# An adaLN transformer layer on 8 cores: every third load of the weight conversion is issued by GpSimd's queue instead of SyncE's

## The reference

```
mod = silu(c) @ wmod                        # six vectors of 1024 per sequence: sa, ca, ga, sb, cb, gb
h = layernorm(x) * (1 + ca) + sa
x = x + ga * attention(h)                   # causal, 8 heads of 128, k and v through a latent of 32
h = layernorm(x) * (1 + cb) + sb
x = x + gb * (shared(h) + routed(h))        # MoE: 8 experts, weights of the top 2; all are computed
shared / expert: (silu(h @ Wgate) * (h @ Wup)) @ Wdown     # 1024 -> 512 -> 1024
```

## Time and profile before

| | us |
|---|---|
| median of 3 runs | 1985.06 |
| all runs | 1984.98, 1985.06, 1988.2 |
| the profiled execution | 1989.04 |
| its span on the slowest core (core 7) | 1987.4 |
| spans of the 8 cores | 1967.9 to 1987.4 |

### The profile page before, as it was taken

How to read it: one execution, slowest core, us unless ns; L and a number is a source line. 1 busy time by engine, 2 the same in 40 slices (tenths; PEclk the granted TensorE clock), 3 DMA queues, 4 the chain that set the end, 5 groups by cost and what they waited for, 6 DMA issues and landing times.

```text
span 1987.4 us, 20612 instructions; the slowest of 8 cores (1967.9 to 1987.4 us)
## 1 busy us (share of the span) xinstructions
PE 1295.3 (65%) x5238; PEld 483.6 (24%) x5238; DVE 687.8 (35%) x1269; ACT 495.5 (25%) x914; POOL 216.1 (11%) x226
## 2 busy tenths in 40 slices
PE   3613245125677622537997998898814499999998
PEld 0111122110021100212332333333302233333333
DVE  0333322343124613323334333234453333443433
ACT  0031312320056324234332432243132210000000
POOL 0002020022345773000000000000000000000000
PEclk8855557557875655656998999899956699999999
DMA  9506040059978775000111112111100012211114
GB/s 276 160 0 187 16 149 11 0 180 281 301 238 246 227 225 165 1 0 22 43 64 64 33 53 64 43 64 64 64 0 1 0 64 75 75 64 64 64 64 190
DMA packets 90437, 193.99 MB, mean 98 GB/s; under 512 B 14184, under 2 KB 14248, under 8 KB 90328
## 3 DMA queue, kind: packets, MB, share of 16 engines
q1 hardware_dynamic: 64848, 130.64, 21.7%
q10 hardware_dynamic: 16648, 33.60, 5.5%
q0 software_dynamic: 8832, 28.45, 3.6%
HBM read 155.92 MB, written 36.70 MB: 97 GB/s over the span
## 4 chain that ended last, share of the span: by engine, by line
PE 57%; DVE 13%; issue 10%; ACT 9%; DMA 8%; DVEq 1%; ACTq 1%; POOL 0%; SPq 0%; POOLq 0%
PE ps L947 14%; PE ps L914 13%; PE ps L929 12%; DMA stage<-wmod 5%; PE ps L1085 4%; PE ps L549 3%; PE ps L450 3%; PE ps L1028 3%; ACT h1b L535 3%; DVE h1b L542 2%; DVE h1b L539 2%; DVE st_sm L502 2%; DMA q_aug<-bbf 2%; PE ps L703 2%; PE ps L604 1%
## 5 line engine op out<-in xcount | busy, mean ns | idle before, releaser
L947 PE MATMUL ps<-down_bf,act_e 128*128 128x512 bf16 x1152 | 288.3, 384 | 34.6 <-DVE act_e L937 12.8
L914 PE MATMUL ps<-hT,gate_bf 128*128 128x512 bf16 x1152 | 285.0, 392 | 19.8 <-ACT r_t L883 13.8
L549 PE MATMUL ps<-ident,h1b 128*128 128x128 f32 x256 | 69.1, 425 | 322.6 <-DVE h1b L542 322.6
L929 PE MATMUL ps<-hT,up_bf 128*128 128x512 bf16 x1152 | 274.8, 382 | 1.4 <-PE ps L914 0.7
L937 DVE TENSOR_TENSOR act_e<-ps,silu_s 128x512 bf16<-128x512 f32 x144 | 99.6, 692 | 419.1 <-PE ps L929 377.5
L956 DVE SCALAR_TENSOR_TENSOR x_res<-ps,comb,x_res 128x512 f32<-128x512 f32 x256 | 192.2, 751 | 147.1 <-PE ps L947 143.5
L923 ACT ACTIVATE silu_s<-ps 128x512 bf16<-128x512 f32 x144 | 86.1, 598 | 516.9 <-PE ps L914 516.8
L1090 ACT ACTIVATE pT<-ps 128x512 bf16<-128x512 f32 (+3 forms) x320 | 159.3, 533 | 159.9 <-PE ps L1085 147.4
L914 PEld LDWEIGHTS ps<-hT,gate_bf 128*128 128x128 bf16 x1152 | 112.9, 100 | 168.4 <-issue 46.4
L947 PEld LDWEIGHTS ps<-down_bf,act_e 128*128 128x128 bf16 x1152 | 96.5, 97 | 221.3 <-issue 144.7
L929 PEld LDWEIGHTS ps<-hT,up_bf 128*128 128x128 bf16 x1152 | 113.0, 99 | 143.5 <-issue 12.0
(11 more groups left out here) (117 smaller groups left out, 833.1 us busy)
## 6 DMA issues: line engine op xcount, KB each, us to landing
stage<-wmod ACTq DMA_DIRECT2D x96, 256.0 KB, 10.8
gate_bf<-wc_g SPq DMA_DIRECT2D x72, 256.0 KB, 4.7
up_bf<-wc_u SPq DMA_DIRECT2D x72, 256.0 KB, 3.4
down_bf<-wc_d SPq DMA_DIRECT2D x72, 256.0 KB, 3.6
pc_in<-w_gate SPq DMA_DIRECT2D x64, 256.0 KB, 5.8
pc_in<-w_up SPq DMA_DIRECT2D x64, 256.0 KB, 4.5
pc_in<-w_down SPq DMA_DIRECT2D x32, 512.0 KB, 4.0
wc_g<-pc_o POOLq DMA_DIRECT2D x36, 256.0 KB, 5.0
```

Of the source, the lines that this page charges most:

```text
L549: tok = P.op("t", lambda e, dc=dc, u=u, pt=pt: e.transpose(pt[:, 128 * u:128 * (u + 1)], h1b[:, 128 * dc:128 * (dc + 1)], ident32[:]), rd= ...
L914: tok = P.op("t", lambda e, buf=buf, hc=hc, qc=qc, dc=dc, psg=psg: e.matmul(psg[:, :], gate_bf[:, buf, dc, 128 * hc:128 * (hc + 1)], hT[:, ...
L929: tok = P.op("t", lambda e, hc=hc, qc=qc, dc=dc, psu=psu: e.matmul(psu[:, :], up_bf[:, dc, 128 * hc:128 * (hc + 1)], hT[:, dc, 512 * qc:51 ...
L947: tok = P.op("t", lambda e, i=i, dch=dch, hc=hc, psd=psd: e.matmul(psd[:, :], act_e[:, hc, 128 * i:128 * (i + 1)], down_bf[:, hc, 512 * dc ...
```

## The change

Unit n takes its load's issuing engine from n mod 3: with n mod 3 = 2 it is POOL ("g"), otherwise SP ("q") as before. Nothing else differs: same transfers, same buffers, same semaphores, same waits.

```diff
--- before.py
+++ after.py
@@ -371,17 +371,18 @@
         def _pc_unit(kind, e_, u):
             islot = _pci[0] % 3
             oslot = _pci[0] % 2
+            qe = "g" if _pci[0] % 3 == 2 else "q"
             _pci[0] += 1
             bi, bo = b_pcin[islot], b_pcout[oslot]
             war = list(bi.r) + ([bi.w] if bi.w else [])
             if kind == "d":
                 if e_ < E:
-                    t_in = P.dma("q", lambda e, e_=e_, u=u, islot=islot: e.dma_start(
+                    t_in = P.dma(qe, lambda e, e_=e_, u=u, islot=islot: e.dma_start(
                         out=pc_in[:, islot, :],
                         in_=dwdown[e_, 128 * u:128 * (u + 1), :]),
                         extra=war, sem="P%d" % islot, serial=False)
                 else:
-                    t_in = P.dma("q", lambda e, u=u, islot=islot: e.dma_start(
+                    t_in = P.dma(qe, lambda e, u=u, islot=islot: e.dma_start(
                         out=pc_in[:, islot, :],
                         in_=dwsd[128 * u:128 * (u + 1), :]),
                         extra=war, sem="P%d" % islot, serial=False)
@@ -391,13 +392,13 @@
                 for h2 in range(2):
                     dc = 2 * u + h2
                     if e_ < E:
-                        t_in = P.dma("q", lambda e, e_=e_, dc=dc, h2=h2, islot=islot,
+                        t_in = P.dma(qe, lambda e, e_=e_, dc=dc, h2=h2, islot=islot,
                                      dsrc=dsrc: e.dma_start(
                             out=pc_in[:, islot, 512 * h2:512 * (h2 + 1)],
                             in_=dsrc[e_, 128 * dc:128 * (dc + 1), :]),
                             extra=war, sem="P%d" % islot, serial=False)
                     else:
-                        t_in = P.dma("q", lambda e, dc=dc, h2=h2, islot=islot,
+                        t_in = P.dma(qe, lambda e, dc=dc, h2=h2, islot=islot,
                                      dsrcs=dsrcs: e.dma_start(
                             out=pc_in[:, islot, 512 * h2:512 * (h2 + 1)],
                             in_=dsrcs[128 * dc:128 * (dc + 1), :]),
```

## The result

| | before | after |
|---|---|---|
| median of 10 runs, us | 1985.28 | 2051.8 |
| profiled execution, us | 1989.04 | 2051.83 |
| its spans on the 8 cores, us | 1967.9 to 1987.4 | 2025.7 to 2050.2 |

The change makes the kernel 3.2% slower: the ratio is 1.0319, 95% interval 1.0305 to 1.0333. The direction and the mechanism held. The size was put at 35 us; it is 67 by the medians and 63 by the ratio, near the upper end of the range.

The account below looks back on a forecast made before the run. The conversion was taken as off the path with 53 us to spare; lengthened rounds bring up_bf at 866 us, a 37.5 us stall less 2.65, net 35, so 1985.06 becomes 2020 us, range 1988 to 2056.

Parts of the forecast that it names:

- the slack: Before PE first uses up_bf at 828.5 us: converted weights are there at 775.5 us, 53 us to spare.
- The loads of wq and wo: On SP behind conversion loads: pushed by at most 16 us each, against slack of 51 and 17 us; costed at nothing.
- A late load is exposed: On POOL, every third load is issued right ahead of its cast and waited for: 28 times, 4 to 6 us each.
- the exposed load of kind d: On POOL ahead of a cast of kind d: 4.8 us per load, in rounds of 14.5 us against 10.3 before.
- units 26 to 38, beside wmod: Conversion on POOL during wmod's loads: 4 rounds of 17.9 us, 71.6 us, with 8.2 us per exposed load.
- The round of g and u: Three units on POOL: load 5.3, cast and wait 1.58, store 3.6, next unit 2.12; 12.6 us against 10.0 before.
- The 2.65 us: PE's wait at 857 us for VectorE's next row tile goes in the stall's shadow, leaving net 35 us of 37.5.
- What the thinner traffic gives: PE's wmod waits and the norms' small loads shrink by 10 to 20 us together, worth nothing ahead of the stall.
- The first: At the first use of up_bf: exposed loads cost at most 2.4 to 3.5 us, no stall, 1985 us; chance 6%.
- The second: Beside wmod and norms: waits shrink by 10 us and the conversion is still in time, 1975 us; chance 8%.
- The third: POOL's loads take 7.7 us everywhere, 2.9 us more for each of 23 exposed loads, 2087 us; chance 10%.
- VectorE's hold on the common port: GpSimd cannot write descriptors while VectorE holds the port; would act in the 2087 us rival's direction, no size given.

Follow-up runs that it names:

- the short conversion: Changed kernel with 24 of the 36 units d left out (outputs not the reference's): 1959.62 us, ratio 0.9834 to the kernel before.
- the moved conversion: Kernel before, all loads on SP, 16 units moved between the first-half norms and wo's loads, none beside wmod: 1955.84 us, ratio 0.9831.

## Why the prediction was right or wrong

**What bounds the kernel, and the slack.** Right. The conversion was off the path, and the kernel is longer by the wait for its end. But line 930 shows 20.4 us of it, not the 30 to 45 that were put there: `gate_dma` stands on SP behind the conversion's last loads, so line 915 waited first. The prediction had not seen that wait; it ends before the one at line 930, so the time is the same. The loads of wq and wo, costed at nothing, cost nothing: PE's first matmul on wmod comes at 455.2 us in the mean, 455.1 before.

**A late load is exposed.** Right, and shown. POOL waits for its own loads 28 times behind 450 us, on core 2 for 3.1 to 7.1 us each behind the wmod stage, where 4 to 6 were put. The same loads two units early left 11 us of the 106 by which the last cast came later, and ahead of the store they cost less.

**The size.** This is the term that was mis-sized: the conversion behind unit 26 was put about 15 us too short, and most of that is the exposed load of kind d. From the issue of the late load of one unit to that of another, in us:

| | put | mean of the cores | core 7 | core 2 |
|---|---|---|---|---|
| units 26 to 38, beside wmod | 71.6 | 70.6 | 70.0 | 72.9 |
| 38 to 41 | 15.3 | 12.7 | 13.3 | 12.8 |
| 41 to 71, ten rounds of g and u | 126.0 | 129.0 | 128.2 | 132.1 |
| 71 to 74 | 13.9 | 15.1 | 15.2 | 15.3 |
| 74 to 107, eleven rounds of d | 159.5 | 173.3 | 172.8 | 172.8 |
| 107 to the first use of `up_bf` | 16.0 | 16.3 | 15.3 | 16.7 |
| sum | 402.3 | 417.0 | 414.7 | 422.6 |

From issue to cast a load of d was put at 4.8 us, the median of POOL's stores of half its size, and took 5.9 in the mean; a load of g or u was put at 5.3 and took 6.1. The round of g and u was still nearly right, by two errors against each other: the store was put at 3.6 us and is not waited for there. That of d had no such cover, since its store was put at nothing. One round of d also shared the DMA engines with the four loads of `gate_bf` and took 17.2 us. Beside wmod 17.9 us a round were put and 17.6 measured.

**The core.** The sum was made on core 7, the slowest in the profile before, and there it looks close: `up_bf` first used at 866 us predicted, 871.6 measured, its span 38.8 us longer with 37.5 less 2.65 predicted. That is luck. The sum from the first late load was 12.4 us too short there, but this load was issued at 456.9 us, 6.8 us sooner than the 463.7 put, as the core reached that stage sooner in this execution. On core 2, the slowest after, the load was issued at 466.87 us and the sum was 20.3 us too short: 889.5 us, 23.5 after the prediction. With no stall before, the time followed the core on which PE came latest; now it follows the one whose conversion ends last, and the first use of `up_bf` is spread over 870.7 to 889.5 us. Which core is the slowest changes from run to run of the changed kernel: cores 0 to 4 all come up. So the 28 us between 2024 and 2051.8 are 20.3 us of the sum, 3.2 of the start and 4 behind the first use. In the mean of the cores the spans grew by 59.5 us and the first use came 60.0 us later.

**What comes back.** Nothing. The 2.65 us were to go in the shadow of the stall; the same wait is there, as long as before, on core 2:

```profile
920.80 1.09 PE L550 MATMUL ps<-ident,h1b 128*128 128x128 f32 x4 [2.65 <-DVE h1b L543]
```

Behind the first use of `up_bf` the spans have 1157.3 us left in the mean before and 1156.8 after. Nor did the profiled execution lie 4 us above the median, as the forecast took over from before: 2051.83 against 2051.8.

**What the thinner traffic gives.** Right, in size too. It was put at 10 to 20 us for wmod and norms together, worth nothing behind the stall: PE's router matmuls are done at 798.5 us in the mean instead of 811.2, 12.7 us sooner. With the short conversion, whose end is out of the way as well, it is 25 us.

**The rivals.** The first, that the slack holds, fell. The second, faster because slack and relief both hold, is not what the change does, but it exists: six late loads are 0.5% faster. The third, POOL's loads as slow everywhere as beside wmod, fell: 5.5 us beside attention, 6.6 and 7.9 beside wmod. VectorE's hold on the common port, named with it from the Trainium skill's page "SBUF — State Buffer", shows no sign here: early loads from POOL landed in 3.5 us in the same stage of the kernel; whether VectorE held the port there, no run shows. The Trainium skill's figure from "DMA: Bandwidth & Descriptors", an estimate of 2.6 us for 256 KB from GpSimd, is met by no median of this case's loads; the nearest is that 3.5, and 5.5 where the load was late. The measured times decide here.

## What to carry to other kernels

A load belongs on a queue whose engine has something else to do until it lands: moving every third one right ahead of its own use cost 3.2%, the same loads two units earlier on the same queue left the time where it was. Work off the path has a due time and a traffic: before it is made slower, find its due time on every core, since the slowest core of one execution need not be that of the next. A near hit on one core is no proof of a sum: compare it stretch by stretch. What is hidden still takes bandwidth from what is not: moving the conversion out of the way of two short stages gave 1.6%.

## What the runs showed of the hardware that was not expected

PE's waits for wmod were 22.4 us, yet without the conversion beside it the stage became 31.6 us shorter in the mean. Much of the rest goes with the clock. The stage on core 7 of the kernel before and on core 5 of the moved conversion (window, length, busy time and count of PE, PEld, DVE, ACT, POOL, then granted clock, DMA share, GB/s):

```profile
459.00:545.30 86.30, 59.24 (x103) 7.19 (x104) 12.82 (x19) 0.00 (x0) 28.51 (x37) 0.83 0.98 311
```

```profile
459.89:512.00 52.11, 45.68 (x104) 8.27 (x102) 13.38 (x21) 0.00 (x0) 1.04 (x1) 0.96 0.77 240
```

The same 96 matmuls and a few more keep PE busy 59.2 us at a mean granted clock of 0.83 and 45.7 us at 0.96. In the kernel before PE was fed in pieces there, and the clock was part of the time at the lower of its two levels, 1.2 GHz (0.50 in the lines), and part at the upper, 2.4 GHz:

```profile
475.00:479.00 4.00, 2.96 (x5) 0.31 (x4) 1.60 (x3) 0.00 (x0) 0.00 (x0) 0.50 1.05 382
487.00:491.00 4.00, 2.44 (x7) 0.29 (x5) 2.24 (x4) 0.00 (x0) 1.59 (x3) 1.00 1.03 326
535.00:539.00 4.00, 2.54 (x6) 0.23 (x4) 0.00 (x0) 0.00 (x0) 1.15 (x2) 1.00 0.97 377
```

Five matmuls took 2.96 us at the lower level, seven 2.44 us at the upper. If the waits brought the clock down, a wait for data was paid twice, once as a wait and once in the matmuls behind it: 13.5 us here beside 22.4 us of waits. That is not shown. The two kernels show only that both went together, and the last two lines have the upper level with PE fed in pieces as well.
